# Two mixes' products issued together as 32-row tiles, and layer 3's stages at new places, in a four-layer attention and RWKV kernel

## The chip, the cores and the metric

The kernel runs on one core of one Trainium2 chip. The metric is the time of one execution in microseconds, as the device gives it. Everything is computed in float32. Five engines run their own instruction streams in order: TensorE (PE; PEld is its weight load), VectorE (DVE), ScalarE (ACT), GpSimd (POOL) and SyncE (SP, which issues DMAs). They wait for one another through semaphores only.

## The reference

`x` is 64 sequences of 64 tokens of 256 features; it goes through four layers. Layers 0 to 2 are attention layers (0: scores over the features' axis with four 64x64 convolutions; 1: grouped queries with 32 heads over 8 key heads, softmax, normalization; 2: 16 heads over context and tokens, softmax, RMS norm, Gelu MLP of 1024). Layer 3 is an RWKV block, and the change lies in it:

```
xa  = layernorm(x);  sx = shift(xa) - xa
xxx = tanh((xa + sx * maa_x) @ maa_w1)                # 5 mixes of 32 values per token
xxx = einsum('blfd,fde->blfe', xxx, maa_w2)           # per mix f: [32] @ [32, 256]
xm  = xa + sx * (maa_stack + xxx)                     # five mixed inputs: k, w, v, r, g
w = exp(-exp(time_decay + tanh(xw @ td_w1) @ td_w2))
r, k, v = xr @ Wr.T, xk @ Wk.T, xv @ Wv.T;  g = silu(xg @ Wg.T)
per head of 8:  out_t = r_t (u * k_t v_t + s);  s = k_t v_t + w_t * s      # 64 steps
og = groupnorm(out);  x1 = x + og * g @ Wo.T
xc = layernorm(x1);  kk = relu(mix_k(xc) @ Wfk.T)^2
return x1 + sigmoid(mix_r(xc) @ Wfr.T) * (kk @ Wfv.T)
```

## The kernel before, in words

**Blocks.** The 64 sequences are cut into 8 groups of 8 (512 tokens). The program is nine blocks. Block g runs layers 0, 1 and 2 of group g and, threaded between them, layer 3 of group g-1. So block 0 has no layer 3, blocks 1 to 7 have all four layers, and the last block has layer 3 of the last group alone. There the group is cut into two halves of 4 sequences whose stages are merged by a list of times, and a ring of six banks is used.

**Order.** Every engine has its own loop over units i (0 to 60), in which layers 0 to 2 are written out: scores, softmax, transposes, products with the values, projections. Then come the eight hidden products of layer 2's MLP (`hidden` and L690: w1) with ACT's Gelus, and its second product (L1097: w2). Between these pieces each engine calls `step()`, twice per unit and once per hidden product. `step()` counts, and issues those stages of layer 3 whose place has come. The places stand in a table, `PLACES` and `SCAN_PLACES`: for every stage four numbers, for PE, ACT, DVE and POOL. Stages whose place comes after the last piece are issued at the block's end. The table sets nothing but the order of instructions on an engine; the time comes from who waits for whom.

**Banks.** PSUM has eight banks of 128x512. `fill` takes the next one of a ring and waits until it was emptied: ring "score" has banks 0 and 1, ring "turn" 2 to 5, ring "late" 6 and 7. Layer 3 beside the others has only ring "late".

**Layer 3's stages.** `moments`, `normalize`, `turn` (PE transposes, L698, ACT copies with the norm's weights), `shift` (DVE: L1440, L1444), `maa` (PE two products of 256x160, ACT tanh into `xf`), five `mix` stages, `td` and `decay` (the decay w), `k`, `v`, `r`, `g` (256x256 products), `r u k` and `bonus`, then 19 scan stages: POOL multiplies keys by values (L1739; the values come by a DMA that spreads them over partitions), DVE scans along the tokens (L1410, `tensor_tensor_scan`) and multiplies by r (L1422), and PE sums with a 0/1 matrix ("pick", L774) into one bank per four pairs. DVE adds the bonus (L1429, `heads`). Then `center` (PE, ACT copy and square), `variance` (PE, ACT logarithm and exponential, for which ACT loads another table, 'natural_log_exp', and then the Gelu table again), `gate` (DVE L1481, L1484), `project` (Wo, L706), the second norm and the three feed-forward products (Wfk, Wfr, Wfv).

**A mix stage.** `xf` holds the tanh results: mixes 0 to 3 in rows 32f to 32f+31 of its first half, mix 4 in rows 0 to 31 of its second. `maa2[:, f, :]` holds the weights of mix f in the same 32 rows and zeros in the other 96. The order of mixes is 1, 0, 2, 3, 4. A stage makes two products over all 128 rows (one per 128 features) into banks 6 and 7. DVE then computes (product + maa_stack) * sx out of each bank (L1388) and adds xa (L1392):

```
for m in range(KT):
    product(own(stage, m), P.tok, [(maa2[:, f, 128 * m:128 * m + 128], P.xf[:, f // 4, :])], P.ring)
```

The seam that the text speaks of is the end of layer 2 in a block, where the last picks, `center` and `variance` stand among the hidden products. The xnT transposes (L880) turn layer 2's normalized c; the hidden products of the first half of tokens (L981, h = 0) need only the first half's xnT. The head is the block's beginning: layer 0's convolutions, scores (L834), its softmax (ACT L1235, POOL L1794), its transposes (L849), and layer 3's turn, shift and maa.

In layer 1 and 2 the scores are already issued side by side: `side_by_side` (L834) gives two products of 64 or of 32 rows to two banks one after the other.

Of the kernel before, what the change touches and what calls it, by code (L numbers as in the profile page):

```python
# [29 lines left out]
KT = E // 128  # L30
# [24 lines left out]
def build(nc, a, out):  # L55

    with ExitStack() as ctx:
# [394 lines left out]
        def clear_all():  # L452
# [26 lines left out]
            "normalize": (4, 5, 1, 0),  # L479
            "turn": (11, 10, 3, 0),  # L480
            "shift": (11, 10, 11, 9),
            "maa": (15, 15, 15, 10),
            "mix 0": (17, 28, 18, 17),
            "mix 1": (22, 28, 24, 28),
            "td": (29, 28, 28, 32),
            "k": (32, 29, 34, 33),
            "mix 2": (35, 29, 34, 33),
            "decay": (39, 36, 37, 36),
            "v": (42, 36, 41, 37),
            "mix 3": (42, 36, 41, 39),  # L490
            "mix 4": (43, 39, 42, 50),
            "r": (46, 43, 43, 50),
            "g": (49, 49, 46, 50),
            "r u k": (52, 50, 50, 50),
            "bonus": (56, 50, 53, 54),
            "center": (125, 125, 121, 118),
            "variance": (127, 127, 124, 126),
            "gate": (130, 129, 124, 126),
            "project": (133, 133, 124, 126),
            "moments 2": (133, 133, 127, 126),  # L500
            "normalize 2": (134, 133, 127, 134),
            "turn 2": (134, 133, 127, 134),
            "shift 2": (135, 137, 127, 134),
            "ffn k": (135, 141, 128, 138),
            "ffn r": (138, 149, 128, 153),
            "ffn v": (147, 154, 146, 156),
        }
        SCAN_PLACES = (
# [50 lines left out]
        def group_block(now, before, after):  # L559
# [122 lines left out]
            def tensor_program(pe):  # L682
# [26 lines left out]
                def layer3(stage, P):  # L709
# [8 lines left out]

                    def square(w, moving):
                        for m in range(KT):  # L720
                            product(own(stage, m), P.tok, [(wt[w][:, k, 128 * m:128 * m + 128], moving(k)) for k in range(KT)], P.ring)
# [1164 lines left out]
```

## Time and profile before

| | |
|---|---|
| three timed runs | 1798.56, 1798.26, 1789.37 us; median 1798.26 |
| the profiled execution | 1787.11 us, its span 1785.3 us |
| mean granted TensorE clock | 0.983 |
| busy: PE, DVE, ACT, POOL | 89%, 68%, 53%, 43% |
| one steady block | about 212 us |
| last block | 105 us |

How to read it: the span runs from the first to the last instruction; the rows below are from the profiled execution. Float32 products appear as two PE records each, so x4 in a timeline is two products of two records. Records overlap by about 0.15 us, and the chain's pieces run from one start to the next. In brackets a timeline row gives the idle time ahead of it and who ended it. "issue" means that the profile shows no one.

### The profile page before, as it was taken

The numbers are of one execution on the slowest core, as the hardware profiler recorded it, in microseconds if no ns is written. First come the engines' busy times: TensorE is split into PE (matmuls) and PEld (weight loads), VectorE is DVE, ScalarE is ACT, GpSimd is POOL, SyncE is SP. The second block draws the span as 40 slices with busy tenths as digits, with TensorE's granted clock in tenths as the row PEclk, the third lists the DMA queues.
The fourth block names the chain that finished last, engine by engine and source line by source line (L and its number), as shares of the span: only waits on it lengthen the run. The fifth ranks groups of instructions, "written<-read, shape, count | busy, mean of one in ns | idle before, by whom it ended". The sixth has DMA issues, their size and how long they took to land.

```text
span 1785.3 us, 35476 instructions
## 1 busy us (share of the span) xinstructions
PE 1584.3 (89%) x13831; PEld 1027.2 (58%) x13831; DVE 1222.6 (68%) x2259; ACT 939.4 (53%) x1922; POOL 769.4 (43%) x882
## 2 busy tenths in 40 slices
PE   5898998899998999898988989889999899989856
PEld 3666555565565755655556655566556565566524
DVE  4743579655795658946699457975579566894496
ACT  4444555555655545556455565555565554564413
POOL 5632248503584146821478024860458314682000
PEclk9999999999999999999999999999999999999978
DMA  6001024200341005210061102420034100520060
GB/s 190 9 1 39 1 25 54 40 23 8 37 56 37 20 1 62 37 31 20 1 73 26 30 20 25 53 51 17 4 39 53 37 20 1 64 35 1 14 92 17
DMA packets 75923, 60.83 MB, mean 34 GB/s; under 512 B 39264, under 2 KB 60912, under 8 KB 75760
## 3 DMA queue, kind: packets, MB, share of 16 engines
q1 hardware_dynamic: 58000, 47.99, 18.6%
q10 hardware_dynamic: 17216, 10.55, 2.1%
q8 instruction: 112, 1.84, 0.4%
q14 instruction: 51, 0.42, 0.1%
q0 software_dynamic: 544, 0.03, 0.0%
HBM read 20.28 MB, written 4.19 MB: 14 GB/s over the span
## 4 chain that ended last, share of the span: by engine, by line
PE 63%; DVE 15%; ACT 10%; issue 6%; POOL 5%; ACTq 1%; DMA 0%; DVEq 0%; SPq 0%; POOLq 0%
PE bank L690 24%; PE bank L834 7%; PE bank L1097 6%; DVE late L1410 5%; PE bank L1034 5%; PE bank L706 3%; PE bank L1059 2%; DVE late L1422 2%; PE bank L967 2%; POOL soft_ring L1786 2%; PE bank L849 2%; PE bank L943 2%; PE bank L774 2%; ACT soft_ring L1250 2%; POOL late L1739 1%
## 5 line engine op out<-in xcount | busy, mean ns | idle before, releaser
L1786 POOL TENSOR_TENSOR soft_ring<-soft_ring,seg_max 128x512 f32<-128x512 f32 x256 | 285.5, 1127 | 259.2 <-DVE seg_max L1576 257.9
L1250 ACT ACTIVATE soft_ring<-soft_ring 128x512 f32<-128x512 f32 x256 | 160.5, 627 | 212.7 <-POOL soft_ring L1786 212.2
L1410 DVE TENSOR_TENSOR_SCAN late<-late 128x520 f32<-128x520 f32 (+1 forms) x128 | 204.7, 1599 | 3.7
L1739 POOL TENSOR_TENSOR late<-late 128x520 f32<-128x520 f32 x112 | 175.4, 1566 | 39.2 <-DVE late L1410 38.4
L1034 PE MATMUL bank<-ident,soft_ring 128*128 128x128 f32 x1024 | 160.6, 284 | 24.3 <-ACT soft_ring L1250 21.7
L1034 PEld LDWEIGHTS bank<-ident,soft_ring 128*128 128x128 f32 x1024 | 111.9, 141 | 102.0 <-ACT soft_ring L1250 47.8
L1576 DVE TENSOR_REDUCE seg_max<-soft_ring 128x8 f32<-128x512 f32 (+1 forms) x256 | 166.5, 674 | 0.2
L1752 POOL COPY late<-edge 128x8 f32<-128x8 f32 (+1 forms) x16 | 3.2, 198 | 336.6 <-DVE late L1514 288.5
L834 PE MATMUL bank<-early 32*128 32x128 f32 (+2 forms) x1024 | 144.5, 402 | 1.3 <-DVE soft_ring L1561 1.1
L1125 ACT ACTIVATE late<-bank 128x512 f32<-128x512 f32 (+4 forms) x103 | 57.9, 571 | 120.8 <-PE bank L690 118.7
L1794 POOL TENSOR_SCALAR soft_ring<-soft_ring,rden 128x256 f32<-128x256 f32 x64 | 59.3, 929 | 139.9 <-DVE rden L1538 139.9
L1097 PE MATMUL bank<-w,early 128*128 128x256 f32 x512 | 113.0, 379 | 0.0
L1561 DVE SCALAR_TENSOR_TENSOR soft_ring<-bank,mask 128x512 f32<-128x512 f32 x128 | 82.1, 682 | 44.2 <-PE bank L834 44.1
L1422 DVE TENSOR_TENSOR late<-late 128x512 f32<-128x512 f32 (+1 forms) x128 | 106.4, 836 | 0.0
L1125 ACT ACTIVATE early<-bank,vec 128x512 f32<-128x512 f32 (+1 forms) x102 | 65.7, 677 | 74.9 <-PE bank L690 53.4
L690 PE MATMUL bank<-late,maa 128*128 128x512 f32 (+3 forms) x224 | 102.9, 586 | 2.4 <-DVE late L1444 1.9
L1097 PEld LDWEIGHTS bank<-w,early 128*128 128x128 f32 x512 | 96.7, 190 | 13.3 <-issue 0.5
L1569 DVE SCALAR_TENSOR_TENSOR soft_ring<-bank,mask 128x512 f32<-128x512 f32 x128 | 82.1, 682 | 30.6 <-PE bank L834 30.6
L834 PEld LDWEIGHTS bank<-early 32*128 32x128 f32 (+1 forms) x1024 | 73.6, 187 | 48.3 <-issue 45.7
L774 PE MATMUL bank<-late,pick 128*32 128x512 f32 (+1 forms) x256 | 67.1, 604 | 32.7 <-DVE late L1422 32.2
L690 PE MATMUL bank<-early,w 128*128 128x512 f32 x160 | 71.9, 597 | 8.7 <-ACT early L1125 8.7
L1125 ACT ACTIVATE early<-bank 128x512 f32<-128x512 f32 (+2 forms) x76 | 42.0, 564 | 67.8 <-PE bank L967 27.4
(327 smaller groups left out, 3417.5 us busy)
## 6 DMA issues: line engine op xcount, KB each, us to landing
late<-late SPq DMA_DIRECT2D x112, 260.0 KB, 4.4
c<-in_ctx ACTq DMA_DIRECT2D x8, 512.0 KB, 4.0
x<-in_x ACTq DMA_DIRECT2D x8, 512.0 KB, 4.9
out_x<-late SPq DMA_DIRECT2D x7, 512.0 KB, 2.9
late<-late SPq DMA_DIRECT2D x16, 130.0 KB, 3.7
early<-early SPq DMA_DIRECT2D x16, 130.0 KB, 3.9
mask<-in_mask_Bx1xSxS_ff ACTq DMA_DIRECT2D x16, 128.0 KB, 4.0
mask<-in_mask_BxS_ik SPq DMA_DIRECT2D x8, 256.0 KB, 3.5
```

The lines of the kernel that those rows point to most:

```text
L690: ins = mm(t[0:lhsT_cols(lhsT), 0:cols], lhsT, rhs, start=n == 0, stop=n == len(terms) - 1)
L774: ins = mm(t[32 * c:32 * c + 32, 0:P.tok], pick[:, e, :, :], P.rs[:, i % RS, :], start=e == 0, stop=e == 1)
L834: ins = mm(t[:, width * n:width * n + width], lhsT, rhs, start=True, stop=True)
L1034: ins = tr(t[:, 128 * n:128 * n + 128], soft[:, u % SOFT, 128 * n:128 * n + 128], ident[:, :])
L1097: ins = mm(t[:, E * (p % 2):E * (p % 2) + E], gT[:, k, 128 * p:128 * p + 128], w2[:, k, :], start=k == 0, stop=k == HID // 128 - 1)
L1125: af(dst, src(t), func, **kw).then_inc(free, 1)
L1250: af(soft[:, u % SOFT, :], soft[:, u % SOFT, :], ACT.Exp).then_inc(sig("exp"), 1)
L1410: nc.vector.tensor_tensor_scan(P.sj[:, n % 2, :], P.wP[:, k, :, :].rearrange("p b t -> p (b t)"), P.aj[:, n % 2, :], 0.0, ALU.mult, ALU.ad ...
L1422: tt(batches(P.rs[:, n % RS, :]), batches(P.rT[:, k, :]), P.sj[:, n % 2, :].rearrange("p (b t) -> p b t", t=LP)[:, :, 0:L], ALU.mult).then ...
L1576: nc.vector.tensor_reduce(seg_max[:, u % SOFT, 0:KVH if u < UNITS else 4], cuts(u, soft[:, u % SOFT, :]), X, ALU.max).then_inc(sig("max"), 1)
L1739: tt(P.aj[:, n % 2, :], P.kP[:, k, :, :].rearrange("p b t -> p (b t)"), P.vj[:, n % P.depth, :], ALU.mult).then_inc(mine("kv_done"), 1)
L1786: tt(s, s, seg_max[:, u % SOFT, 0:segs].unsqueeze(2).broadcast_to([128, segs, 512 // segs]), ALU.subtract).then_inc(sig("sub"), 1)
```

## The change

Two things change. First, mixes 1 and 0, and mixes 3 and 4, are made in pairs. Stage "mix 0" makes the products of both mixes for the first 128 features, stage "mix 1" those for the last 128, each product over the 32 rows that hold its values, one into bank 6 and the other into 7. The same holds for stages "mix 3" and "mix 4". On DVE each stage scales its two products; the sums (L1399 in the changed kernel) of both mixes are all made in the second stage. Mix 2 stays as it was. Second, the tables of places have other numbers; some of them move no instruction past another.

```
+                    def mix_two(n, m):
+                        for f in (MIXES[n], MIXES[n + 1]):
+                            r = slice(32 * (f % 4), 32 * (f % 4) + 32)
+                            t, full = fill(pe, P.ring, own("mix", f, m))
+                            mm(t[:, 0:P.tok], maa2[r, f, 128 * m:128 * m + 128], P.xf[r, f // 4, :], start=True, stop=True).then_inc(full, 1)
...
-                        mix(MIXES[int(stage[4])])
+                        n = int(stage[4])
+                        if n == 2:
+                            mix(MIXES[n])
+                        else:
+                            mix_two(*{0: (0, 0), 1: (0, 1), 3: (3, 0), 4: (3, 1)}[n])
...
+                    def mix_two(first, k):
+
+                        for n in (first, first + 1):
+                            if k == 0 and n:
+                                filled({1: own("maaB"), 3: own("k", 1), 4: own("v", 1)}[n])
+                            scaled(own("mix", MIXES[n], k), n, k)
+                        if k == KT - 1:
+                            for n in (first, first + 1):
+                                for j in range(KT):
+                                    shifted(own("mix", MIXES[n], j), n, j)
...
-            "turn": (11, 10, 3, 0),
-            "shift": (11, 10, 11, 9),
-            "maa": (15, 15, 15, 10),
+            "turn": (6, 8, 5, 2),
+            "shift": (9, 9, 9, 8),
+            "maa": (13, 13, 12, 8),
...
-            "center": (125, 125, 121, 118),
-            "variance": (127, 127, 124, 126),
+            "center": (128, 126, 123, 133),
+            "variance": (129, 129, 123, 137),
```

Here `scaled` is the old L1388 of one tile and `shifted` the old L1392 of one tile.

**Seam, PE.** From the last pick but one to the Wo projection (`pick`: scan read-out; `w`: hidden weights, or w1; `same`: variance; in the changed kernel L774 is L784 and L981 is L991). Before:

```order
L774 MATMUL bank<-late,pick 32x512 x2
L690 MATMUL bank<-wo,early 128x256 x2
L774 MATMUL bank<-late,pick 32x512 x2
L690 MATMUL bank<-late,center 128x512 x2
L981 MATMUL bank<-early,w 128x256 x6
L880 MATMUL bank<-ident,c 128x128 x4
L981 MATMUL bank<-early,w 128x256 x4
L690 MATMUL bank<-late,same 128x512 x2
L981 MATMUL bank<-early,w 128x256 x2
L690 MATMUL bank<-early,w 128x512 x10
L706 MATMUL bank<-t_Wo,late 128x256 x8
```

And now:

```order
L784 MATMUL bank<-late,pick 32x512 x2
L690 MATMUL bank<-wo,early 128x256 x2
L991 MATMUL bank<-early,w 128x256 x6
L890 MATMUL bank<-ident,c 128x128 x4
L991 MATMUL bank<-early,w 128x256 x2
L784 MATMUL bank<-late,pick 32x512 x2
L991 MATMUL bank<-early,w 128x256 x4
L690 MATMUL bank<-late,center 128x512 x2
L690 MATMUL bank<-early,w 128x512 x2
L690 MATMUL bank<-late,same 128x512 x2
L690 MATMUL bank<-early,w 128x512 x8
L706 MATMUL bank<-t_Wo,late 128x256 x8
```

The last pick and `center` stand behind hidden products of both halves, and `variance` (`same`) behind them and one w1 product. On ACT, center's four passes and variance's moved with them, behind the xnT copies and the loads' issue and between the Gelus.

**Head, PE.** From the first scores of layer 0 up to the first mix (`late`, `maa` products are layer 3's; L849 is L859, L834 is L844 and L858 is L868 in the changed kernel). Before:

```order
L834 MATMUL bank<-early 128x256 x8
L849 MATMUL bank<-ident,soft_ring 128x128 x4
L698 MATMUL bank<-ident,late 128x128 x8
L834 MATMUL bank<-early 128x256 x4
L849 MATMUL bank<-ident,soft_ring 128x128 x8
L858 MATMUL bank<-early 64x256 x4
L690 MATMUL bank<-late,maa 128x512 x2
L690 MATMUL bank<-late,maa 32x512 x2
L834 MATMUL bank<-early 128x256 x4
L849 MATMUL bank<-ident,soft_ring 128x128 x4
```

And now:

```order
L844 MATMUL bank<-early 128x256 x4
L698 MATMUL bank<-ident,late 128x128 x8
L844 MATMUL bank<-early 128x256 x4
L859 MATMUL bank<-ident,soft_ring 128x128 x4
L844 MATMUL bank<-early 128x256 x4
L859 MATMUL bank<-ident,soft_ring 128x128 x4
L690 MATMUL bank<-late,maa 128x512 x2
L690 MATMUL bank<-late,maa 32x512 x2
L859 MATMUL bank<-ident,soft_ring 128x128 x4
L868 MATMUL bank<-early 64x256 x4
L844 MATMUL bank<-early 128x256 x4
L859 MATMUL bank<-ident,soft_ring 128x128 x4
```

The turn's transposes stand between the first two pairs of scores instead of behind a softmax tile's transposes, and maa stands one softmax tile earlier and ahead of a value product. In both kernels mix 0 follows; the paired mixes' line is L723.

**Mixes 3 and 4, DVE.** Between two units' masks of layer 1 (L1561 is L1590, L1576 is L1605). Before:

```order
L1561 SCALAR_TENSOR_TENSOR soft_ring<-bank,mask 128x512 x2
L1576 TENSOR_REDUCE seg_max<-soft_ring 128x8
L1388 SCALAR_TENSOR_TENSOR late<-bank,vec,late 128x512 x2
L1392 TENSOR_TENSOR late<-late 128x512 x2
L1576 TENSOR_REDUCE seg_max<-soft_ring 128x8
L1388 SCALAR_TENSOR_TENSOR late<-bank,vec,late 128x512 x2
L1392 TENSOR_TENSOR late<-late 128x512 x2
L1561 SCALAR_TENSOR_TENSOR soft_ring<-bank,mask 128x512 x2
```

And now:

```order
L1590 SCALAR_TENSOR_TENSOR soft_ring<-bank,mask 128x512 x2
L1605 TENSOR_REDUCE seg_max<-soft_ring 128x8 x2
L1393 SCALAR_TENSOR_TENSOR late<-bank,vec,late 128x512 x4
L1399 TENSOR_TENSOR late<-late 128x512 x4
L1590 SCALAR_TENSOR_TENSOR soft_ring<-bank,mask 128x512 x2
```

Four products are scaled in a row and then four sums are made; on PE the group of transposes that stood between the two mixes stands behind both.

## Rows read from the trace of the kernel before

**Rows 1.** page, part 1: busy us (share), instructions of each engine
```profile
PE 1584.3 (89%) x13831; PEld 1027.2 (58%) x13831; DVE 1222.6 (68%) x2259; ACT 939.4 (53%) x1922; POOL 769.4 (43%) x882
```

**Rows 2.** windows, a steady block and the last: PE, PEld, DVE, ACT, POOL, clock, DMA
```profile
1052.00:1264.00 212.00, 194.10 (x1716) 124.70 (x1712) 150.48 (x259) 117.41 (x238) 99.29 (x107) 1.00 0.21 32
...
1680.00:1785.00 105.00, 69.12 (x280) 43.28 (x280) 79.22 (x225) 32.61 (x76) 3.35 (x13) 0.80 0.30 46
```

**Rows 3.** chain that ended last: start us, us, what; stretch 1044 to 1256
```profile
1058.20 1.72 PE bank L690 x4
...
1092.07 1.06 PE bank L834 x4
1093.13 0.59 PE bank L1034 x4
...
1097.15 0.44 PE bank L1034 x4
```

**Rows 4.** timeline of PE, seam; start us, us, engine, line, operation, xcount, [idle before <- releaser]
```profile
1189.89 1.13 PE L690 MATMUL bank<-wo,early 128*128 128x256 f32 x4
1192.27 1.05 PE L774 MATMUL bank<-late,pick 128*32 128x512 f32 x4 [1.25 <-DVE late L1422]
...
1195.14 2.75 PE L981 MATMUL bank<-early,w 128*128 128x256 f32 x12
...
1199.26 1.99 PE L981 MATMUL bank<-early,w 128*128 128x256 f32 x8 [0.93 <-ACT early L1310]
...
1208.62 5.42 PE L690 MATMUL bank<-early,w 128*128 128x512 f32 x12 [1.35 <-ACT early L1125]
1213.87 3.62 PE L706 MATMUL bank<-t_Wo,late 128*128 128x256 f32 x16
```

**Rows 5.** timeline of ACT, seam
```profile
1196.49 1.28 ACT L1110 ACT_TABLE_LOAD   x1
1198.36 0.84 ACT L1310 ACTIVATE early<-bank,vec 128x256 f32<-128x256 f32 x2 [0.59 <-PE bank L880]
...
1201.68 1.27 ACT L1125 ACTIVATE early<-bank,vec 128x512 f32<-128x512 f32 x2 [2.48 <-issue]
...
1204.26 1.27 ACT L1125 ACTIVATE late<-bank,eps 128x512 f32<-128x512 f32 x2
```

**Rows 6.** timeline of DVE, seam
```profile
1193.97 0.60 DVE L1602 TENSOR_SCALAR c<-xr,rstd 128x256 f32<-128x256 f32 x2
1206.16 1.41 DVE L1481 SCALAR_TENSOR_TENSOR late<-late,vec 128x512 f32<-128x512 f32 x2 [11.58 <-ACT late L1188]
1207.49 1.41 DVE L1484 SCALAR_TENSOR_TENSOR late<-late,vec 128x512 f32<-128x512 f32 x2
```

**Rows 7.** timeline of PE, head of the next block
```profile
1253.42 0.63 PE L849 MATMUL bank<-ident,soft_ring 128*128 128x128 f32 x4 [2.38 <-POOL soft_ring L1794]
...
1257.87 0.63 PE L849 MATMUL bank<-ident,soft_ring 128*128 128x128 f32 x4 [1.29 <-issue]
...
1259.45 3.82 PE L690 MATMUL bank<-late,maa 128*128 128x512 f32 x8
```

**Rows 8.** timeline of DVE, head of the next block
```profile
1255.41 1.29 DVE L1440 TENSOR_TENSOR late<-late 128x512 f32<-128x512 f32 x2 [0.97 <-ACT late L1125]
1256.62 1.41 DVE L1444 SCALAR_TENSOR_TENSOR late<-late,vec 128x512 f32<-128x512 f32 x2
```

**Rows 9.** timelines of PE and DVE, mixes 3 and 4
```profile
1087.93 1.98 PE L690 MATMUL bank<-late,maa 128*128 128x512 f32 x4
1089.75 0.60 PE L1034 MATMUL bank<-ident,soft_ring 128*128 128x128 f32 x4
...
1089.08 1.62 DVE L1388 SCALAR_TENSOR_TENSOR late<-bank,vec,late 128x512 f32<-128x512 f32 x2 [3.09 <-PE bank L690]
```

**Rows 10.** timeline of PE, first scans
```profile
1121.80 0.66 PE L880 MATMUL bank<-ident,c 128*128 128x128 f32 x4 [1.05 <-DVE c L1598]
```

**Rows 11.** chain that ended last, last block
```profile
1684.52 12.95 PE bank L690 x56
```

More of the change, by code:

```diff
@@ L1379, in own, with scaled, shifted, mix @@
                         return (P.tag, *tile)
-                    def mix(n, f):
-                        if n:
-                            filled({1: own("maaB"), 2: own("td"), 3: own("k", 1), 4: own("v", 1)}[n])
+                    def scaled(tile, n, k):
+                        t, free = take(dve, tile)
+                        stt(out=P.xm[:, (n + 1) % 2, k, :], in0=t[:, 0:P.tok], scalar=v("maa", 2 * MIXES[n] + k), in1=P.sx[:, k, :],
+                            op0=ALU.add, op1=ALU.mult).then_inc(free, 1)
+                    def shifted(tile, n, k):
+                        drained(dve, tile)
+                        m = P.xm[:, (n + 1) % 2, k, :]
+                        tt(batches(m), batches(m), P.xaP[:, k, :, 1:LP], ALU.add).then_inc(mine("xm_ready"), 1)
+                    def mix(n):
+                        filled(own("td"))
                         for k in range(KT):
-                            t, free = take(dve, own(stage, k))
-                            m = P.xm[:, (n + 1) % 2, k, :]
-                            stt(out=m, in0=t[:, 0:P.tok], scalar=v("maa", 2 * f + k), in1=P.sx[:, k, :], op0=ALU.add, op1=ALU.mult).then_inc(free, 1)
+                            scaled(own(stage, k), n, k)
                         for k in range(KT):
-                            drained(dve, own(stage, k))
-                            m = P.xm[:, (n + 1) % 2, k, :]
-                            tt(batches(m), batches(m), P.xaP[:, k, :, 1:LP], ALU.add).then_inc(mine("xm_ready"), 1)
+                            shifted(own(stage, k), n, k)
+                    def mix_two(first, k):
[7 more added lines that the diff above has]
+                                    shifted(own("mix", MIXES[n], j), n, j)
                     def weighted(n):
@@ L1447, in layer3 @@
                         n = int(stage[4])
-                        mix(n, MIXES[n])
+                        if n == 2:
+                            mix(n)
+                        else:
+                            mix_two(*{0: (0, 0), 1: (0, 1), 3: (3, 0), 4: (3, 1)}[n])
                     elif stage == "r u k":
```

46 lines of the change are left out of this document (23 added, 23 removed), and 8 rows, old and new, of the table SCAN_PLACES.

## The prediction

> **What bounds the kernel now.** I read the page first. TensorE (PE) is busy for 1584.3 of 1785.3 us, 89% of the span; nothing else is near [rows 1]. The windows by block say that this is no single limit. One steady block of 212 us has 194.1 us of PE work, so PE stands still for 18 us of it; the granted clock is 1.00 throughout, which is the 2.4 GHz level. The last block, which has no other layers beside it, is different: 69.1 us of PE work in 105 [rows 2]. The chain that ended last then gives prices, since its pieces run from start to start: two mixing products cost 1.72 us, two 64-row products side by side, of the same 512 columns each, 1.06 us, and the transposes behind such a pair 0.59 us where the same transposes elsewhere take 0.44 [rows 3]. Last I read PE's timeline with its waits at the three places where the order of rows differs. At the seam (layer 2's end beside layer 3's end) PE waits 1.25 us for the scan's last reads on VectorE (DVE), 0.93 us for ScalarE's (ACT's) copy of xnT, and 1.35 us for a Gelu [rows 4]. At the head (layer 0's scores) it waits 2.38 us for the first scaled softmax tile and 1.29 us for a later one [rows 7]. Around mixes 3 and 4 it doesn't wait visibly [rows 9].
>
> **The change, part by part.** Everything below is per block, and the seven blocks in which layer 3 runs beside the others repeat the pattern.
>
> *Seam.* Removed from PE's path: the read-out product ("pick") and the two center products now stand behind six, later twelve, of the hidden products. PE is free at 1191.02 (1192.27 less its 1.25 of idle) and can begin the hidden products of the first half at once, since their xnT is long there. They take 2.6 us (2.75 less the 0.15 by which records overlap) [rows 4], so to 1193.6. The transposes need c from DVE. DVE wrote it from 1193.97 on, behind the heads' addition, which is now behind it [rows 6]; I take 1194.3 for its end, so PE idles 0.7 us. The transposes end at 1194.9, and ACT, which no longer has four center passes in front, has its table (1.28 us) loaded by then; its two copies take 0.84 us [rows 5], and PE goes on at 1195.9 after 1.0 us of idle. From 1199.26 to 1213.87 PE did 14.61 us, 1.35 of them idle [rows 4], so 13.26 us of work; with the pick (0.98) and center (1.9) behind them it is 16.1, and the Wo projection starts at 1212.0 instead of 1213.87. By the other count: 3.53 us of waits go, 1.7 come. **Seam: -1.8 us.** What could be late next is the gate. Center starts near 1199.5 now. From there center, four ACT passes, variance, a table load (1.28), logarithms (1.27), exponentials (about 1.0) and four DVE operations (twice 1.41) follow one another [rows 5, 6], some 11 us, so ready at 1210.5: 1.5 us to spare before the projection. The Gelu behind the variance's two table loads comes at about 1209.5, and its bank is wanted again only after the projection.
>
> *Head.* The turn's transposes (eight records, about 0.87 us) move in front of the 2.38 us wait, and maa (3.75 us) moves in front of a softmax tile for which PE waited 1.29 us [rows 7]. The wait of 2.38 is ended by the chain scores, maximum, exponential, scale, which the move doesn't touch, so 0.87 us come off behind it. Maa, however, needs DVE's shift, 2.6 us of DVE that begin behind ACT's two copies of the turned tiles [rows 8]. ACT now makes those copies before the third exponential, DVE is done at about 1256.6 and maa starts at 1256.65, after 0.25 us of idle. That would be 1.25 us at the first mix. But ACT and DVE hold up the later exponentials by some 2.7 us of moved work, and the last of them frees a bank that PE waits for between mix 0 and mix 1. At that point I keep **-1.0 us**, mix 0's own saving included.
>
> *Mixes 0 and 1.* Each stage now issues two 32-row products of two different mixes to banks 6 and 7. I take the price from the 64-row pair: 1.06 + 0.15 behind it, against 1.72 [rows 3], -0.51 a stage. Both banks are empty by then, with other products between the stages. Mix 0's share is in the head; **mix 1: -0.5 us**. The bounds are 0 (they don't overlap) and -0.86 (a pair costs what one costs). DVE's work is the same, but the sums that td waits for now come behind four scaled products instead of two; by the order of rows td's sum is ready at about the moment PE arrives, and the keys' copy behind it on DVE is 1.3 us later, which is hidden by the several us until the first scores. I cost both at nothing.
>
> The Trainium skill, "TensorE: Matmul & The Clock Gate", Part 3, gives the span of packed row tiles as one product's duration plus about 4 ns a tile. By that the pair would cost 0.86 and save 0.86 us; the 64-row row here disagrees (1.06 and 0.15 behind), and the sum goes by the row.
>
> *Mixes 3 and 4.* Here all four pairs of products follow the values' products at once, and the ring has two banks. Call T the values' end (1087.93). In the kernel before, the second product of mix 3 waited about 0.1 us for ACT to empty the values' second bank: 1.82 us from its start to the next instruction's, instead of 1.72 [rows 3, 9]. So the pair's second member can't start before T+0.96 while the first starts at T: they don't overlap. Bank 6 comes free when DVE has scaled the first (DVE began at T+1.15 and one takes 0.7 [rows 9]), T+1.85; bank 7 at T+2.85; the fourth product ends at T+3.7. Before, the same four with one group of transposes between ended at T+4.1 [rows 3]; now the transposes come behind, T+4.3, 0.2 us later. DVE then makes four sums at once, and the products for r wait for the second of them, 0.15 more. **+0.35 us.** Bounds: -1.0 if both pairs overlap, +0.7 if a second DVE operation more is on the path.
>
> *The rest.* Scan stages on POOL and DVE move by a place or two, among subtractions. Between 1110 and 1190 PE waits for DVE work such as c [rows 10], and the amount of DVE and POOL work is the same; one subtraction chain gets 1 us earlier and another 0.9 later. Zero, between -0.7 and +1.0. In the last block the chain has 56 PE records in a row, 12.95 us [rows 11], among them four adjacent pairs that could save 0.3 each; but r there waits for DVE's sums, which now come after more scaling. Zero, between -1.5 and +1 for the whole block.
>
> **Sum.** -1.8 - 1.0 - 0.5 + 0.35 = -2.95 us a block, times seven is -21 us. The profiled execution took 1787.1 us, so 1766. The median of the three timed runs is 1798.3, 11 us above it, and the lowest run 1789.4; on the scale of the median the forecast is **1777 us**. A measurement here tells 0.5%, 9 us, from no change.
>
> **Rivals.** *A: the evacuation sets the pace.* The mixes gain nothing anywhere and mixes 3 and 4 cost their upper bound: seam -1.8, head without mix 0 -0.5, +0.7, so -1.6 a block, -11 us, 1787. For it: ring of two banks, and a DVE pass of 0.7 a product [rows 9]. Against: between mix 0 and mix 1 other products cover the drains. The Trainium skill, "TensorEngine Tiling (Array Packing)", PSUM Bottleneck, says that tiling speeds up TensorE and not the evacuation; for mixes 3 and 4 the rows say the same, for 0 and 1 no row does.
> *B: nothing lasts.* The seam's and head's gains are given back in the 1110 to 1190 stretch, where PE waits for DVE [rows 10], because POOL's and DVE's new order costs there its bound of +1.0, and the seam yields only its first wait less the new ones: about -0.5 a block, -4 us, 1794. Against: the stretch starts when PE has fed it, so what comes earlier in a block should shift it whole.
> *C, slower: the gate is late.* Place: the Wo projection. If the chain from center to gate takes more than 12.5 us instead of my 11, PE waits; from 14.3 on the seam is no gain, and at 18 us (ACT holding variance behind Gelus, Gelus behind tables) a block costs 2.3 us more than before: +16 us, 1814. Against: in the kernel before ACT went through the same work with PE waiting only 1.35.
> *D: more than forecast.* All three waits at the seam go (-3.5), the head gives its 1.3 and mixes 3 and 4 overlap: -6 a block, -42 us, 1756.
>
> **Chances.** Forecast (-14 to -30 us) 0.52, A 0.20, B 0.13, C 0.07, D 0.08. Faster by over 0.5%: the forecast, D and nearly all of A, 0.77; within 0.5%: B and a bit of A, 0.16; slower 0.07. The range leaves out C and the far end of D, and takes in that the median of the runs shown lies 9 us above its lowest: 1758 to 1791.
>
> **What would show it.** Right: in PE's timeline at the seam no wait for the scan's read before the hidden products, two waits of about 1 us around the xnT transposes, and the Wo projection without a wait; the new product line in pairs of about 1.1 us for mixes 0 and 1 but about 3.7 us for the four pairs of mixes 3 and 4; the maximal clock as before; a block of about 208.7 us. Wrong: a wait for DVE's gate before the projection (C), a pair at 1.7 us in mix 0 (A), or a stretch from the first scan to the last that is longer than before by what the seam gained (B).

## The result, and the profile after

The changed kernel takes **1813.01 us** (median of seven runs, 1805.34 to 1816.47); the kernel before, run seven times beside it, 1794.34 us. The ratio is **1.0098, 95% interval 1.0071 to 1.0124**: slower by 1%, where 1777 us was forecast. In a second comparison the ratio was 1.0125. The profiled execution took 1805.34 us, its span 1803.6 us, against 1785.3 us before: 18.3 us more. The page of the profile after, part 1 (busy us, share, instructions) and the row of the granted clock in 40 slices from part 2:

```profile
PE 1623.6 (90%) x13831; PEld 1042.7 (58%) x13831; DVE 1225.6 (68%) x2259; ACT 933.7 (52%) x1922; POOL 768.4 (43%) x882
...
PEclk9999998999999999999989999899999999999778
```

PE has the same 13831 instructions as in [rows 1] and is busy for 39.3 us more; the sums of DVE, ACT and POOL move by 5.7 us at most. So the same products took longer. The mean granted clock says why: 0.955 against 0.983. It is no chance of the profiled execution: all seven runs of the changed kernel have 0.950 to 0.957, and the fast runs of the kernel before, over all comparisons, 0.968 to 0.984. As the clock has two levels, 1.2 and 2.4 GHz, 2 x 0.045 x 1803.6 = 162 us of the span ran at the lower one, against 2 x 0.017 x 1785.3 = 61 us before. A slice of the page is 45 us wide and hides where; a steady block and five of its stretches show it, as windows of the profile after (start:end, length, then busy us and instructions of PE, PEld, DVE, ACT, POOL, granted clock, DMA share, GB/s):

```profile
1044.00:1252.00 208.00, 193.83 (x1671) 122.09 (x1668) 144.71 (x243) 112.34 (x229) 98.44 (x98) 0.96 0.20 29
...
1092.00:1098.00 6.00, 5.74 (x16) 2.09 (x16) 3.54 (x6) 3.72 (x7) 0.78 (x1) 0.91 0.00 0
1098.00:1104.00 6.00, 6.00 (x19) 2.79 (x16) 4.19 (x7) 0.70 (x2) 2.04 (x2) 0.80 0.00 0
1128.00:1134.00 6.00, 4.42 (x18) 3.10 (x20) 5.90 (x7) 2.05 (x5) 5.87 (x6) 0.76 0.39 44
1146.00:1152.00 6.00, 4.53 (x30) 2.40 (x27) 4.69 (x8) 1.42 (x3) 5.47 (x8) 0.68 0.51 63
1206.00:1212.00 6.00, 6.00 (x18) 3.00 (x18) 0.69 (x1) 0.69 (x1) 0.68 (x4) 0.72 0.76 218
```

In the kernel before a steady block stood at 1.00 throughout [rows 2]. Now it has falls at four places (a fall is a stretch at the lower level). PE's timeline of the profile after, right behind the values' products (start us, us, engine, line, operation, count, [idle before <- releaser]), shows the first:

```profile
1092.69 1.88 PE L723 MATMUL bank<-late,maa 32*128 32x512 f32 x4
1094.83 1.78 PE L723 MATMUL bank<-late,maa 32*128 32x512 f32 x4 [0.26 <-DVE late L1393]
1096.54 0.76 PE L1044 MATMUL bank<-ident,soft_ring 128*128 128x128 f32 x4
1097.24 2.08 PE L844 MATMUL bank<-early 64*128 64x512 f32 x4
1099.25 1.11 PE L1044 MATMUL bank<-ident,soft_ring 128*128 128x128 f32 x4
1100.16 3.70 PE L690 MATMUL bank<-late,t_Wr 128*128 128x512 f32 x8
...
1128.51 0.65 PE L890 MATMUL bank<-ident,c 128*128 128x128 f32 x4 [1.82 <-DVE c L1627]
...
1130.67 3.35 PE L964 MATMUL bank<-hT,wq 128*128 128x256 f32 x8 [1.07 <-DVE early L1613]
...
1147.82 1.80 PE L844 MATMUL bank<-early,qm_first 32*128 32x128 f32 x16 [1.47 <-DVE soft_ring L1598]
```

The four products of mixes 3 and 4 are spaced as forecast. But the 64-row scores behind them (L844) take 2.08 us where the same form takes 1.13 at full clock, and the transposes 1.11 instead of 0.6. Later the queries of layer 2 take 3.35 instead of 1.99, behind a wait of 1.82 and one of 1.07, and scores 1.80 instead of 1.16 behind one of 1.47. No wait named here is 2 us long. The seam of the same block, in PE's timeline:

```profile
1199.72 1.13 PE L690 MATMUL bank<-wo,early 128*128 128x256 f32 x4
1200.69 2.75 PE L991 MATMUL bank<-early,w 128*128 128x256 f32 x12
1204.19 0.66 PE L890 MATMUL bank<-ident,c 128*128 128x128 f32 x4 [0.75 <-DVE c L1631]
1205.78 1.72 PE L991 MATMUL bank<-early,w 128*128 128x256 f32 x4 [0.93 <-ACT early L1320]
1207.42 1.92 PE L784 MATMUL bank<-late,pick 128*32 128x512 f32 x4
1209.28 2.13 PE L991 MATMUL bank<-early,w 128*128 128x256 f32 x8
1211.25 1.88 PE L690 MATMUL bank<-late,center 128*128 128x512 f32 x4
...
1223.26 3.62 PE L706 MATMUL bank<-t_Wo,late 128*128 128x256 f32 x16
```

The waits went as forecast: 3.53 us of [rows 4] gone, 0.75 and 0.93 come. But the pick took 1.92 us instead of 1.05, and from the output projection in front (L690 `wo`) to the Wo projection it is 23.54 us, 0.44 less than in [rows 4], not 1.8. In the two blocks behind this one the clock holds at this place, and the same way is 21.94 us, 2.04 less. At the head, also PE's timeline of the profile after:

```profile
1262.82 0.63 PE L859 MATMUL bank<-ident,soft_ring 128*128 128x128 f32 x4 [1.16 <-POOL soft_ring L1823]
...
1266.17 3.82 PE L690 MATMUL bank<-late,maa 128*128 128x512 f32 x8
...
1273.58 1.13 PE L723 MATMUL bank<-late,maa 32*128 32x512 f32 x4
1274.63 0.66 PE L859 MATMUL bank<-ident,soft_ring 128*128 128x128 f32 x4
1275.69 1.09 PE L868 MATMUL bank<-early 128*64 128x256 f32 x8 [0.40 <-ACT soft_ring L1245]
```

The wait of 2.38 us of [rows 7] is 1.16, and a pair of 32-row products costs 1.05 us to the next instruction's start.

Where the 18.3 us lie, by the starts of each block's first convolution and of the Wo projections in PE's timeline: block 0 is 1.8 us shorter; the six blocks behind it take 1285.3 us instead of 1272.1, so +13.3; the last block with all layers is 0.8 shorter up to its Wo projection; what follows, mostly layer 3 of the last group alone, is 7.6 us longer. For that last part, PE's timeline of the profile after and two windows:

```profile
1687.07 2.08 PE L723 MATMUL bank<-late,maa 32*128 32x256 f32 x8 [0.46 <-ACT late L1135]
1690.78 1.97 PE L690 MATMUL bank<-late,td 128*64 128x256 f32 x4 [1.63 <-DVE late L1399]
...
1705.32 3.78 PE L690 MATMUL bank<-late,t_Wr 128*128 128x256 f32 x8 [1.54 <-DVE late L1399]
```

```profile
1682.70:1696.70 14.00, 11.91 (x37) 7.12 (x38) 5.42 (x16) 3.71 (x9) 0.84 (x9) 0.59 0.04 2
1696.70:1710.70 14.00, 12.46 (x49) 7.87 (x47) 8.20 (x23) 5.58 (x13) 0.00 (x0) 0.78 0.01 1
```

The kernel before had 0.87 and 1.00 in the two windows at the same distance from its last full block, a wait of 0.38 us where there are 1.63 now, and none in front of `t_Wr`.

### The profile page after: what moved, and what is told of

Its sections match the earlier page's. It is cut to its first block, busy times and chain, and to the rows that moved or that the text cites. A ratio compares the mean times of both kernels' runs of the same rounds, so it can differ in the third digit from the quotient of the medians.

```text
span 1803.6 us, 35476 instructions
## 1 busy us (share of the span) xinstructions
PE 1623.6 (90%) x13831; PEld 1042.7 (58%) x13831; DVE 1225.6 (68%) x2259; ACT 933.7 (52%) x1922; POOL 768.4 (43%) x882
## 4 chain that ended last, share of the span: by engine, by line
PE 69%; DVE 12%; ACT 11%; issue 5%; POOL 2%; DMA 0%; ACTq 0%; DVEq 0%; SPq 0%; POOLq 0%
PE bank L690 25%; PE bank L844 8%; PE bank L1107 6%; PE bank L1044 5%; PE bank L706 3%; PE bank L977 3%; ACT soft_ring L1245 3%; PE bank L1069 3%; PE bank L784 2%; PE bank L964 2%; PE bank L1062 2%; DVE late L1436 2%; PE bank L723 2%; PE bank L953 2%; PE bank L991 1%
## 5 line engine op out<-in xcount | busy, mean ns | idle before, releaser
L1815 POOL TENSOR_TENSOR soft_ring<-soft_ring,seg_max 128x512 f32<-128x512 f32 x256 | 279.3, 1105 | 284.4 <-DVE seg_max L1605 283.0
L1436 DVE TENSOR_TENSOR_SCAN late<-late 128x520 f32<-128x520 f32 (+1 forms) x128 | 197.0, 1539 | 3.2 <-DVE late L1448 0.5
L1044 PE MATMUL bank<-ident,soft_ring 128*128 128x128 f32 x1024 | 166.9, 292 | 7.1 <-ACT soft_ring L1260 3.7
L1605 DVE TENSOR_REDUCE seg_max<-soft_ring 128x8 f32<-128x512 f32 (+1 forms) x256 | 165.5, 675 | 0.2
L1044 PEld LDWEIGHTS bank<-ident,soft_ring 128*128 128x128 f32 x1024 | 117.5, 146 | 82.5 <-issue 45.3
L844 PE MATMUL bank<-early 32*128 32x128 f32 (+2 forms) x1024 | 151.5, 414 | 1.9 <-DVE soft_ring L1590 1.0
L1590 DVE SCALAR_TENSOR_TENSOR soft_ring<-bank,mask 128x512 f32<-128x512 f32 x128 | 82.2, 684 | 56.0 <-PE bank L844 55.9
L1448 DVE TENSOR_TENSOR late<-late 128x512 f32<-128x512 f32 (+1 forms) x128 | 111.7, 877 | 0.1
L1107 PEld LDWEIGHTS bank<-w,early 128*128 128x128 f32 x512 | 96.7, 190 | 13.3 <-issue 0.5
L844 PEld LDWEIGHTS bank<-early 32*128 32x128 f32 (+1 forms) x1024 | 74.0, 188 | 47.9 <-issue 45.8
L784 PE MATMUL bank<-late,pick 128*32 128x512 f32 (+1 forms) x256 | 74.9, 669 | 15.4 <-DVE late L1448 14.9
L1266 ACT ACTIVATE early<-bank 128x512 f32<-128x512 f32 x128 | 75.1, 586 | 11.3 <-PE bank L1044 11.3
L1269 ACT ACTIVATE early<-bank 128x512 f32<-128x512 f32 x128 | 74.6, 583 | 3.5 <-PE bank L1044 3.5
```

The lines of the kernel that those rows point to most:

```text
L784: ins = mm(t[32 * c:32 * c + 32, 0:P.tok], pick[:, e, :, :], P.rs[:, i % RS, :], start=e == 0, stop=e == 1)
L844: ins = mm(t[:, width * n:width * n + width], lhsT, rhs, start=True, stop=True)
L1044: ins = tr(t[:, 128 * n:128 * n + 128], soft[:, u % SOFT, 128 * n:128 * n + 128], ident[:, :])
L1107: ins = mm(t[:, E * (p % 2):E * (p % 2) + E], gT[:, k, 128 * p:128 * p + 128], w2[:, k, :], start=k == 0, stop=k == HID // 128 - 1)
L1436: nc.vector.tensor_tensor_scan(P.sj[:, n % 2, :], P.wP[:, k, :, :].rearrange("p b t -> p (b t)"), P.aj[:, n % 2, :], 0.0, ALU.mult, ALU.ad ...
L1448: tt(batches(P.rs[:, n % RS, :]), batches(P.rT[:, k, :]), P.sj[:, n % 2, :].rearrange("p (b t) -> p b t", t=LP)[:, :, 0:L], ALU.mult).then ...
```

## The experiments

Two ideas were put to the test first. **Theory N**: the narrow, 32-row products bring the clock down. **Rival P**: the new places do. Each kernel below has one profiled execution, from which its falls are told; its ratio is from all its runs. Four quantities are read in each profile, as distances in PE's timeline: *r*, from the values' first product to r's first (9.05 us before); *v*, from the block's start to the values' (53.31); *seam*, from layer 2's first queries to the Wo projection (90.30); and the length of a steady block (211.67). All ratios are against the kernel before on the same chip.

**One half each.** The first kernel is the changed one with `PLACES` and `SCAN_PLACES` of before; the second is the kernel before with the tables of the change, so all mixes unpaired.

```
-            "turn": (6, 8, 5, 2),
+            "turn": (11, 10, 3, 0),
...
```

> The places of the kernel before with the paired mixes of the change. Theory N (the 32-row pairs of mixes 3 and 4 bring the granted clock to 0.5 behind them, block after block): the clock falls some 60 us into each block here too, the way from the values' products to the r products is about 11.1 us instead of 9.05, and the time is 8 to 20 us above the kernel before. Rival P (the moved stages cause the clock's falls and the loss): clock about 0.98 as before, v to r at most 9.5 us, time within 5 us of before or below it.

Measured: 1800.44 us, ratio 1.0036 (1.0016 to 1.0056), clock 0.971. r is 9.75 in six blocks and 10.78 in one, the only one with a fall behind mixes 3 and 4. Theory N in this plain form is a miss. But at the old places the four narrow products don't stand together; PE's timeline has transposes between them:

```profile
1094.93 1.88 PE L723 MATMUL bank<-late,maa 32*128 32x512 f32 x4
1096.74 0.66 PE L1044 MATMUL bank<-ident,soft_ring 128*128 128x128 f32 x4
1097.33 1.53 PE L723 MATMUL bank<-late,maa 32*128 32x512 f32 x4
```

> The new places with the mixes of the kernel before. Theory N: mean granted clock about 0.98, no fall at 60 us into a block; seam and head keep their gains (1.5 and about 0.7 us a block), so 10 to 18 us below the kernel before. Rival P: clock about 0.955, falls at the same places, time 10 to 20 us above the kernel before.

Measured: 1791.26 us, ratio 0.9979 (0.9957 to 1.0001), clock 0.965. No fall behind mixes 3 and 4 (r 9.35), but falls in the scan stretch; blocks 210.3 to 212.5 us. Neither half alone makes 1%.

**The narrow products alone.** In the changed kernel the products go over all 128 rows again; order, banks and waits stay.

```
-    mm(t[:, 0:P.tok], maa2[r, f, 128 * m:128 * m + 128], P.xf[r, f // 4, :], ...)
+    mm(t[:, 0:P.tok], maa2[:, f, 128 * m:128 * m + 128], P.xf[:, f // 4, :], ...)
```

> The changed kernel with its pairs in the same order and banks, but each product over all 128 rows (the other 96 rows of weights are zeros, the result is the same). Theory N: the rows are what counts, so no fall of the clock behind mixes 3 and 4, v to r about 9.5 us, mixes 0 and 1 cost 0.5 us more each; 8 to 16 us below the kernel before. Rival O (order and waits of the pairs, not their rows, let the clock fall): clock 0.955 and v to r about 11 us as in the changed kernel, time 15 to 25 us above before.

Measured: 1796.31 us, ratio 1.0029 (1.0008 to 1.0049), clock 0.967; r 9.51, no fall there, falls in the scan stretch stay. In the one full block of the changed kernel whose clock did not fall behind mixes 3 and 4 (start 1466.00), r was 9.52, in the others 11.0 to 11.1. So both forms take the same time at full clock, and the narrow one is followed by the fall.

**Only mixes 0 and 1 paired**, with the new places:

```
-    if n == 2:
+    if n >= 2:
         mix(n)
```

> The changed kernel with mixes 3 and 4 made as in the kernel before (128 rows, unpaired), at the changed places; mixes 0 and 1 stay paired. Theory N: clock 0.98, v to r about 9.5 us, 12 to 20 us below the kernel before. Rival P: no better than the changed kernel, 10 to 20 us above before.

Measured: 1785.83 us, ratio 0.9967 (0.9949 to 0.9985), clock 0.968: faster than before. r 9.35, no fall there; v 52.09. In this kernel and the two ahead of it theory N has the clock behind mixes 3 and 4 right, and forecast too short a time, since it allowed for no falls in the scan stretch.

**The change again, its mirror, and the places cut in two.** The first is the changed kernel itself; the second pairs mixes 3 and 4 only (`if n <= 2: mix(n)`).

> The changed kernel as it is, on this chip, as the yardstick for the three beside it. If the slowdown belongs to the kernel and not to one chip, the ratio to the kernel before is again 1.007 to 1.012, the mean granted clock about 0.955, and the clock falls behind mixes 3 and 4 in nearly every block (the r projection 11.1 us behind the values). If it belonged to the chip of the first measurement, the ratio would be under 1.004.

Measured: 1814.93 us, ratio 1.0125 (1.0095 to 1.0154), clock 0.952; r 10.9 to 11.1 in all seven blocks. The slowdown repeats.

> The mirror of the fourth kernel: the new places, mixes 0 and 1 each as one 128-row product after the other, mixes 3 and 4 as 32-row pairs. Theory N (32-row pairs right behind the values' products bring the clock down there): the clock falls about 60 us into nearly every block, the r projection starts 11.1 us behind the values, and the block is 1.6 us longer than with all mixes unpaired, so 7 times 1.6, 11 us, over the second kernel's 0.998: ratio 1.004 to 1.009. Rival M (it needs both, since the pairs of mixes 0 and 1 set how the activity falls on what comes later): the clock stays up there, 9.5 us from the values to r, ratio 0.997 to 1.000.

Measured: 1804.47 us, ratio 1.0059 (1.0036 to 1.0083), clock 0.960; r between 11.06 and 12.29 in six of seven blocks. Theory N's number; the pairs of mixes 0 and 1 are not needed for the fall.

Then the fourth kernel with one part of the places undone each: the scan rows,

```
         SCAN_PLACES = (
-            (63, 49, 64, 55), (63, 52, 65, 63), (64, 52, 67, 66), (65, 54, 69, 66), (70, 57, 70, 66),
+            (63, 52, 64, 58), (63, 54, 67, 65), (64, 54, 67, 66), (65, 61, 67, 67), (71, 61, 69, 67),
...
```

and the last three scan rows with all stages from `center` on.

> The fourth kernel (only mixes 0 and 1 paired, 0.9967) with the scan stages of layer 3's work at their places of before; head and seam stay new. Theory P-scan (the clock falls in and behind the scan stretch because the new scan places leave TensorE waiting in longer pieces there): the falls 94 to 115 us into a block are gone, mean granted clock over 0.975, ratio 0.990 to 0.994. Rival P-seam (they come from the new seam): falls at the seam stay, clock 0.965 to 0.97, ratio 0.995 to 0.999.

Measured: 1780.33 us, ratio **0.9931** (0.9905 to 0.9957), clock 0.972. Three of seven blocks have no fall at all.

> The fourth kernel with the last three scan rows and everything from center on at the places of before; head and scan stretch stay new. The seam's saving of about 1.8 us a block is gone, which costs 12 us, 0.7%, and the head keeps its own. P-seam: no falls at the seam any more, clock over 0.975, which gives back 1 to 2 us a block, ratio 0.994 to 0.999. P-scan: falls at 94 to 115 us stay, ratio 1.000 to 1.004.

Measured: 1800.03 us, ratio 1.0036 (1.0013 to 1.0060), clock 0.964; falls in the scan stretch in every block. So the new scan order brings the second loss of clock, and the new seam, undone here, was a gain of about 0.7%. Windows of one block of the fourth kernel (new scan order), and of one of the kernel with the old scan order, each 90 to 118 us into its block:

```profile
487.00:515.00 28.00, 25.18 (x177) 15.36 (x174) 22.45 (x30) 9.69 (x20) 22.02 (x22) 0.82 0.56 67
```

```profile
1120.00:1148.00 28.00, 23.50 (x190) 15.57 (x189) 26.49 (x34) 11.70 (x23) 23.47 (x22) 1.00 0.57 68
```

And PE's timeline where layer 2 begins. With the new scan order, first the same block as in the window, then one whose clock holds here:

```profile
486.35 0.66 PE L890 MATMUL bank<-ident,c 128*128 128x128 f32 x4 [1.83 <-DVE c L1627]
...
488.51 3.75 PE L964 MATMUL bank<-hT,wq 128*128 128x256 f32 x8 [1.07 <-DVE early L1613]
492.19 1.92 PE L784 MATMUL bank<-late,pick 128*32 128x512 f32 x4
...
1118.96 0.66 PE L890 MATMUL bank<-ident,c 128*128 128x128 f32 x4 [1.83 <-DVE c L1627]
...
1121.12 1.97 PE L964 MATMUL bank<-hT,wq 128*128 128x256 f32 x8 [1.06 <-DVE early L1613]
1123.90 1.05 PE L784 MATMUL bank<-late,pick 128*32 128x512 f32 x4 [0.81 <-DVE late L1448]
```

With the old order:

```profile
1115.15 0.66 PE L1044 MATMUL bank<-ident,soft_ring 128*128 128x128 f32 x4 [0.72 <-ACT soft_ring L1260]
...
1119.33 0.66 PE L890 MATMUL bank<-ident,c 128*128 128x128 f32 x4 [1.05 <-DVE c L1627]
...
1121.10 1.99 PE L964 MATMUL bank<-hT,wq 128*128 128x256 f32 x8 [0.67 <-ACT hT L1291]
1124.31 1.05 PE L784 MATMUL bank<-late,pick 128*32 128x512 f32 x4 [1.22 <-DVE late L1448]
```

The idle time is the same, 3.70 and 3.66 us. The new order bunches it: half of it is one wait, with 1.06 us more right behind. In this cut of the old order there are four shorter ones, and the clock stays up. With the new order it falls here in six blocks of seven, although all seven have the first of these waits; so the waits don't settle it alone.

**The changed kernel with the old scan order:**

> The changed kernel with one part undone: the scan stages of layer 3's work at their places of before. All four pairs, new head and new seam stay. Two causes that add (32-row pairs behind the values; new scan places): the falls in and behind the scan stretch mostly go, the fall behind mixes 3 and 4 stays in nearly every block (r 11.1 us behind the values), ratio 1.000 to 1.005. One cause (the new scan order sets all falls): r 9.5 us behind the values, clock over 0.97, ratio 0.991 to 0.996.

Measured: 1796.39 us, ratio 1.0014 (0.9992 to 1.0036), clock 0.967; r 10.5 to 11.7 in six of seven blocks. Two causes that add.

**Filler.** If bunched idleness is the cause, work added inside the wait should keep the clock up.

```
+    bank = fill(pe, "turn", ("lT", h))
+    for n in range(8):
+        tr(bank[0][:, 128 * (n % 4):128 * (n % 4) + 128], ident[:, :], ident[:, :])
     pe.wait_ge(sig("xh1_ready"), past("xh1_ready") + 2 * h + 2)
...
```

> The fourth kernel (mixes 0 and 1 paired, new scan order, 0.9967) with work added and none removed: eight transposes of the identity into the bank of layer 2's input before TensorE waits for that input (1.83 us there), and four into the bank of layer 2's queries before the next wait (1.06 us). They take about 1.1 and 0.6 us, inside the waits. Theory G (the falls in the scan stretch come from idle TensorE bunched in that wait): the falls 94 to 115 us into a block go, clock over 0.972, and the kernel gets faster though it does more: ratio 0.989 to 0.994. Rival T (the falls come from what the other engines do at that time, or the filler is simply in the way): falls stay, ratio 0.997 to 1.003.

Measured: 1788.36 us, ratio 0.9970 (0.9953 to 0.9988), clock 0.976. PE's timeline:

```profile
1119.07 1.04 PE L1011 MATMUL bank<-ident 128*128 128x128 f32 x8
1121.07 0.66 PE L890 MATMUL bank<-ident,c 128*128 128x128 f32 x4 [0.96 <-DVE c L1632]
```

The wait is filled, and the falls 90 to 115 us into the block went from eleven in seven blocks to two. The time did not follow: the queries start 0.42 us later, and seven falls come further back in the block, up to the seam, where there was one; the average of *seam* is 90.4 us in both kernels. Theory G holds for the place of the falls and failed for the gain.

> The same filler in the kernel with mixes 0 and 1 paired and the old scan order (0.9931), which has few falls there. Theory G: little left to win, ratio 0.990 to 0.994, and the few falls in blocks 3 and 4 go. Rival T: the filler costs up to 0.5 us a piece, ratio 0.994 to 0.999.

Measured: 1779.92 us, ratio 0.9915 (0.9884 to 0.9946), clock 0.980; within the intervals the same as without filler. Its blocks are a scale for the price of a fall: the three without one take 209.62 to 209.83 us, three with one fall each 211.40 to 211.97. One fall is 1.9 us here.

> All places of before, and only mixes 0 and 1 paired. It gives the value of the pairs alone, apart from the places: 0.5 us a stage, 0.9 us a block for the two, 6 to 7 us in all, so ratio 0.995 to 0.998 if the clock stays as before (0.98). If 32-row pairs bring falls at any place, the clock is under 0.975 and the ratio 0.999 to 1.004.

Measured: 1793.18 us, ratio 1.0003 (0.9983 to 1.0024), clock 0.975. The block without a fall takes 210.99 us, 0.7 less than before, and v is 52.44, 0.87 less; but there are nine falls in the seven blocks, where the kernel before has two, and nothing is left of the gain in the median. Neither expectation as a whole: the pair's gain is there, and so is some loss of clock. Four of the nine begin at layer 2's first queries, though the scan order is the old one and the waits in front are those of the old order:

```profile
485.60 0.66 PE L890 MATMUL bank<-ident,c 128*128 128x128 f32 x4 [1.05 <-DVE c L1627]
...
487.36 3.68 PE L964 MATMUL bank<-hT,wq 128*128 128x256 f32 x8 [0.68 <-ACT hT L1291]
```

With these waits the kernel before, the one with the old scan order and the one with full rows have no fall here in any block. So bunching alone doesn't decide it.

**Rows or waits?** On the base with the old scan order, once more the question what in mixes 3 and 4 does it: a 128-row product put in front of each 32-row product there, into the same bank; and all products over 128 rows.

```
+    if n:
+        mm(t[:, 0:P.tok], maa2[:, f, 128 * m:128 * m + 128], P.xf[:, f // 4, :], start=True, stop=True)
     mm(t[:, 0:P.tok], maa2[r, f, 128 * m:128 * m + 128], P.xf[r, f // 4, :], start=True, stop=True).then_inc(full, 1)
```

> The changed kernel with the old scan order (1.0014), and in mixes 3 and 4 each 32-row product has the same product over all 128 rows in front of it, into the same bank, which it then overwrites. Theory N (the small activity of 32-row products brings the clock down): no fall behind mixes 3 and 4, r starts 9.9 to 10.5 us behind the values (part of the four added products of 0.43 us hides in the waits for banks 6 and 7) instead of 11.1, and the kernel gets faster though it does more: ratio 0.993 to 0.999. Rival W (the order and the waits bring it down): the falls stay and the added work comes on top, r 11.5 to 13 us behind, ratio 1.003 to 1.012.

Measured: 1822.92 us, ratio 1.0150 (1.0113 to 1.0188), clock 0.969. The fall behind mixes 3 and 4 is gone from every block (window 1104 to 1118: clock 1.00), as Theory N said; the time is a miss. An added product takes 1.06 us, not 0.43 (that was one record of two), nothing of it hides, and r comes 13.90 us behind the values: 9.52 and four times 1.06, with 0.14 over.

> The changed kernel with the old scan order and all eight products of mixes 0, 1, 3 and 4 over all 128 rows, in the same order and into the same banks, so that no two can overlap by their rows. Theory N: no fall behind mixes 3 and 4, r 9.5 us behind the values, the values themselves 0.5 us later than with 32-row pairs, ratio 0.993 to 0.998. Rival W: r 11.1 us behind, ratio 1.002 to 1.006.

Measured: 1788.58 us, ratio 0.9961 (0.9945 to 0.9977), profiled span 1781.0, clock 0.982. Windows of this kernel and of the one with narrow products and the same order, 55 to 69 us into a block:

```profile
1081.00:1095.00 14.00, 13.94 (x46) 5.99 (x45) 9.14 (x16) 7.59 (x15) 3.69 (x4) 1.00 0.01 1
```

```profile
452.00:466.00 14.00, 13.74 (x44) 5.76 (x43) 8.66 (x14) 6.68 (x13) 2.54 (x3) 0.88 0.00 0
```

r is 9.51 in every block. Of the full blocks only the first has falls; the five behind it take 209.88, 209.89, 210.06, 209.88 and 209.88 us. Without falls the blocks repeat to 0.2 us, and 1.8 us below those of before.

The two causes crossed, all with mixes 0 and 1 in pairs:

| ratio to before | new scan order | old scan order |
|---|---|---|
| mixes 3 and 4 as 32-row pairs (the change) | 1.0098, 1.0125 | 1.0014 |
| the same order, 128 rows (mixes 0 and 1 too) | 1.0029 | 0.9961 |
| mixes 3 and 4 unpaired, 0 and 1 as 32-row pairs | 0.9967 | 0.9931 |

The new scan order costs 0.4 to 1.1% in each row; narrow products, against full ones in the same order, 0.5 to 1% in each column, although they save 0.54 us a block at mixes 0 and 1.

## Why the prediction was wrong

**The step that failed** stood at the end, as a thing to check: "the maximal clock as before". Every duration of the sum was one at the 2.4 GHz level, and no rival had a clock that falls. The sum's 1766 us on the profile's scale was missed by 39 us: the six blocks between the first and the last with all layers were to save 17.7 us and lost 13.3, and the last part lost 7.6. A block of this order without falls would take at most about 208.9 us. This is an estimate from rows: 92.11 up to the first queries in the one block without a fall behind mixes 3 and 4, 87.77 from there to the Wo projection in the shortest block with the new places (only mixes 0 and 1 paired; a fall reaches 1.6 us into this stretch), and 28.99 behind it. It is 2.8 us below before, where 2.95 were forecast. The measured blocks take 211.3 to 215.2, so the falls cost some 32 us in the six. At full clock the sum was right to 0.2 us a block, with some luck: its terms were off by 0.1 to 0.3 us each, some up, some down.

**Seam, -1.8.** Right in its waits, and -2.04 where the clock stays up (21.94 us against 23.98); with the old scan order it is -1.69 (22.29). In the block shown above the fall left -0.44.

**Head -1.0 and mix 1 -0.5.** v is 1.2 us earlier, forecast 1.5. The places give 0.67 (the runs with full rows), the pairs 0.54; at the old places the pairs alone gave 0.87. A pair costs 1.05 on its row, as taken; of the gain of mix 0's two stages, waits for ACT's scaled tiles behind them (0.40 us in the rows after) take part back.

**Mixes 3 and 4, +0.35.** Measured +0.47 at full clock: 0.30 from the places (it is there with unpaired mixes too), 0.17 from the order of the four products. The rows of mixes 3 and 4 are those forecast. What followed, 1.6 us lost at 1.2 GHz in nearly every block, was not.

**The scan stretch, zero.** Right at full clock, by two shifts that cancel: from r to the first queries it is 0.48 us longer than before (30.49 against 30.01), and from there to the output projection ahead of the seam 0.49 shorter (65.83 against 66.32). That another order of the same waits could cost the clock was not asked.

**The last block, zero.** The mechanism was named (td and r wait for DVE's sums behind more scaling) and priced at nothing; it is 1.25 us for td (1.63 less 0.38) and 1.54 for r. With the clock at 0.59 and 0.78 that became 7.6. The likeness to the steady blocks, where other layers' products hide those sums, was the mistake: here there are none. The same last part is 5.3 us longer than before with all products over 128 rows in the same order, and 1.7 us with unpaired mixes at the new places (one profiled execution each). So most of the loss comes with the paired order; how the waits bring the clock down there is not shown.

**Rivals.** The sign was C's, the mechanism not: center started at 1211.25, the gate was written at 1222.05, 10.8 us later (11 forecast), 1.2 us ahead of the Wo projection. Of A, that mixes 3 and 4 gain nothing from their tiles holds; mixes 0 and 1 do gain.

**How far the cause is shown.** That the lost time is clock is shown: the same instructions take 1.6 to 1.9 times as long in just the stretches with a lower granted clock, and blocks without falls repeat. That four 32-row products in a row behind the values bring it about is shown too: two pairs of kernels differ in the rows of the products alone. It takes the four together, or something else in the new places, since at the old places one block of seven fell. It stays open whether the rows themselves or the small pauses of narrow products do it, since the full rows also have no visible 0.26 us wait, and the filler product took both away. That the new scan order costs clock and time is shown by two pairs of kernels; in the third, with mixes 3 and 4 unpaired, the intervals overlap, but the mean clocks don't (0.964 to 0.970 against 0.972 to 0.975). That it does so by bunching the waits is argued only: for it speaks the filler, which took the falls away from this place, though not the lost time; against it the kernel with all old places and mixes 0 and 1 paired, which fell at the same place in four of seven blocks with unbunched waits, and the changed kernel with the old scan order, which did so in two. One rival is untested. The same rows fall in one block and not in another of the same kernel, so something beyond the order of instructions takes part, perhaps when a block begins; no run here varies that by itself.

The Trainium skill, "TensorE: Matmul & The Clock Gate", in the part on a second failure mode, tells of a kernel whose PE paused for moments between groups of products as it cycled through PSUM banks, so that the clock went to and fro. The traces agree in this: falls stand behind waits of 0.26 to 1.83 us here. The same page of the Trainium skill, in Part 1, puts the cost of the ramp (the time at the lower clock before it rises) under 1% of a typical kernel's span. That is said of the ramp when a kernel starts, and it can't be carried over to a kernel that falls again in each block: here the time at the lower level went from 61 to 162 us, and the result by 1%.

## What to carry to other kernels

A kernel whose matmul engine is busy for 90% at full clock can lose more by a few short falls per period than a change saves; compare the granted clock by windows, not over the whole span, before any instruction is counted at its old duration. Fewer rows in a product saved nothing here where its neighbour couldn't run beside it, and cost clock; the pairs that met two empty banks saved 0.54 us a block. When work is reordered, an unchanged sum of waits says nothing of the clock: measure it again. Here the pairs of mixes 0 and 1, the new head and the new seam, with the old scan order and unpaired mixes 3 and 4, give 0.9931, faster than both kernels.

## What was not expected of the hardware

- The clock fell in six of seven blocks behind four 32-row products with a single wait of 0.26 us among them, and in none behind four 128-row products in the same order (r 11.1 against 9.51 us).
- The same rows with the same waits fell in some blocks and not in others: with waits of 1.05 and 0.68 us ahead of layer 2's first queries, in four blocks of seven in one kernel and in none in the kernel before.
- One fall cost a block 1.9 us (the old scan order with filler).
- Two 32-row products next to each other cost 1.05 us when their banks are empty, and one 32-row product between two full ones costs the same 1.05 (1105.63 to 1106.68 in the kernel with added full products): the row height alone saves nothing.
